# Quantizing x's row tiles every 18 pieces from step 127 on, in place of once per unit

## The reference

```python
xn = layernorm(x)                       # x: 4 x 512 x 512
s = attention(xn, wq, wk, wv, wo)       # 32 query heads of 16, one key and value head, causal
h = linear8bit(xn, W1, b1)              # 512 -> 2048
g = silu(linear8bit(h, W2, b2))         # 2048 -> 512
out = x + s * g
```

## Time and profile before

| | |
|---|---|
| median of 3 runs | 774.07 us (772.74 to 776.4) |
| profiled execution | 773.78 us |
| its span, first to last instruction | 772.1 us |
| TensorE busy | 736.0 us (95%) |
| VectorE busy | 635.6 us (82%) |
| ScalarE busy | 398.3 us (52%) |
| GpSimd busy | 295.6 us (38%) |
| granted TensorE clock, mean | 0.997 |

### The profile page before, as it was taken

The page is one execution under the profiler, slowest core; times in us unless marked ns, Lnnn a source line. Parts: engine busy times, 40 slices in busy tenths (PEclk is TensorE's granted clock), DMA queues, the critical chain, the costliest instruction groups (busy, mean ns, idle before and its releaser), DMA issues. The chain is left out here.

```text
span 772.1 us, 11989 instructions
## 1 busy us (share of the span) xinstructions
PE 736.0 (95%) x4133; PEld 560.6 (73%) x4133; DVE 635.6 (82%) x1080; ACT 398.3 (52%) x681; POOL 295.6 (38%) x369
## 2 busy tenths in 40 slices
PE   4998999999999999999999999999998999999995
PEld 3887765656666777765678878788876888888884
DVE  7878999998999999995548588597869998599957
ACT  4653566766676777777634445454463333132312
POOL 7557445555555555554622222122100000127404
PEclk9999999999999999999999999999999999999998
DMA  7542123222323333344455766555315588337972
GB/s 259 161 168 60 40 54 88 72 73 85 85 85 91 97 90 90 86 122 144 145 191 155 205 218 183 184 118 151 83 44 195 199 257 271 124 93 252 323 287 109
DMA packets 93772, 110.71 MB, mean 143 GB/s; under 512 B 43136, under 2 KB 50320, under 8 KB 92176
## 3 DMA queue, kind: packets, MB, share of 16 engines
q1 hardware_dynamic: 93712, 109.95, 46.8%
HBM read 56.43 MB, written 40.37 MB: 125 GB/s over the span
## 5 line engine op out<-in xcount | busy, mean ns | idle before, releaser
L1024 DVE TENSOR_REDUCE rowmax<-ps 128x2 f32<-128x512 f32 (+3 forms) x384 | 211.5, 589 | 20.4 <-PE ps L1137 18.0
L946 ACT ACTIVATE probs<-ps 128x512 f32<-128x512 f32 (+1 forms) x352 | 174.4, 561 | 66.5 <-PE ps L1152 65.3
L1137 PE MATMUL ps<-km,stack 128*128 128x256 f32 (+3 forms) x512 | 142.5, 325 | 2.8 <-PEq L236 2.1
L1152 PE MATMUL ps<-stack,ks 128*128 128x512 f32 (+1 forms) x352 | 131.8, 383 | 4.4 <-ACT probs L946 3.4
L1137 PEld LDWEIGHTS ps<-km,stack 128*128 128x128 f32 (+1 forms) x512 | 92.2, 189 | 36.6 <-DVE rowmax L1024 19.4
L899 POOL TENSOR_SCALAR_AFFINE_SELECT probs<-probs 128x512 f32<-128x512 f32 x128 | 80.6, 638 | 55.8 <-ACT probs L946 55.0
L2019 PE MATMUL ps<-big_h 128*128 128x512 f32 x256 | 100.0, 390 | 2.0 <-DVE big_l L1835 1.6
L2020 PE MATMUL ps<-big_l,big_h 128*128 128x512 f32 x256 | 99.6, 389 | 0.0
L2021 PE MATMUL ps<-big_h,big_l 128*128 128x512 f32 x256 | 99.6, 389 | 0.0
L1167 PE MATMUL ps<-probs,vones 128*32 128x512 f32 (+3 forms) x1024 | 82.2, 439 | 0.2 <-POOL probs L899 0.2
L1152 PEld LDWEIGHTS ps<-stack,ks 128*128 128x128 f32 x352 | 66.4, 189 | 14.4 <-ACT probs L946 7.2
(11 more groups left out here) (234 smaller groups left out, 1377.6 us busy)
## 6 DMA issues: line engine op xcount, KB each, us to landing
stack<-big_h SPq DMA_DIRECT2D x128, 64.0 KB, 2.0
h_scratch<-hs SPq DMA_DIRECT2D x7, 1024.0 KB, 4.7
hload<-h_scratch SPq DMA_DIRECT2D x14, 512.0 KB, 5.3
xn_scratch<-xa SPq DMA_DIRECT2D x4, 1024.0 KB, 4.6
stack<-big_l SPq DMA_DIRECT2D x64, 64.0 KB, 2.0
xi<-xn_scratch SPq DMA_DIRECT2D x16, 256.0 KB, 2.7
xe_scratch<-xm SPq DMA_DIRECT2D x16, 256.0 KB, 2.3
w2n<-in_L_ffn_W_dram SPq DMA_DIRECT2D x4, 1024.0 KB, 6.7
```

The costliest lines, as they stand in the source:

```text
L946: nc.scalar.activation(probs[p][:, o:o + nh * w], ps[:, STB[n % NST], 0:nh * w], ACT.Exp).then_inc(s_exp, 1)
L1024: nc.vector.tensor_reduce(dst, src, AX_X, ALU.max).then_inc(s_red, 1)
L1137: last = nc.tensor.matmul(dst, stack[u % 3][rows, hp, P * qt:P * (qt + 1)], km[rows, u // KT, p0:p0 + npar, keys], start=True, stop=True)
L1152: ins = nc.tensor.matmul(ps[:, STB[n % NST], 0:nh * w].rearrange("p (h q) -> p h q", h=nh), ks[:, u // KT, p, P * kt:P * (kt + 1)], stack[ ...
```

## The change

The tiles no longer go with the units. Tile i is loaded at step 128 + 18i, masked at 136 + 18i, scaled at 139 to 142 + 18i, rounded at 143 + 18i, scaled back at 145 + 18i and stored at 147 + 18i. The reload of a stored tile in the tail (line 825) follows the last store. Engines, operations, buffers and semaphores stay.

```diff
--- before.py
+++ after.py
@@ -645,7 +645,8 @@
         PV_AT = {11: (0, 0), 16: (0, 1), 22: (1, 0), 27: (1, 1)}
         NORM_AT = {19: 0, 27: 1, 30: 2, 33: 3}
         SHARE_AT, HIGH_AT, LOW_AT = 30, 34, 33
-        XLOAD_AT, XMASK_AT, XSCALE_AT, XROUND_AT, XBACK_AT, XSTORE_AT = -1, 15, 21, 25, 26, 30
+        XFIRST, XSTEP = 127, 18
+        XLOAD_AT, XMASK_AT, XSCALE_AT, XROUND_AT, XBACK_AT, XSTORE_AT = 1, 9, 12, 16, 18, 20
 
         LATE_AT = {("kv", LAST, 0): 0, ("q", LAST, 0): 6, ("q", LAST, 1): 12, ("v", LAST, 0): 18,
                    ("q", LAST, 2): 18, ("q", LAST, 3): 24}
@@ -675,6 +676,10 @@
 
             t = g - CH - LAG - at
             return t // CH if t % CH == 0 and 0 <= t < CH * U else -1
+
+        def x_tile_at(g, at):
+            i, r = divmod(g - XFIRST - at, XSTEP)
+            return i if r == 0 and 0 <= i < NT else -1
 
         def maximized(g, after):
 
@@ -803,12 +808,12 @@
                 queries(1)
                 queries(2)
                 for g in range(STEPS):
-                    u = unit_at(g, XLOAD_AT)
+                    u = x_tile_at(g, XLOAD_AT)
                     if u >= 0:
                         if u:
                             sp.wait_ge(s_xt, u)
                         sp.dma_start(xi[:, :], xn_d[P * u:P * (u + 1), :]).then_inc(s_xl, 16)
-                    u = unit_at(g, XSTORE_AT)
+                    u = x_tile_at(g, XSTORE_AT)
                     if u >= 0:
                         sp.wait_ge(s_xe, u + 1)
                         sp.dma_start(xe_d[P * u:P * (u + 1), :], xm[:, :]).then_inc(s_xes, 16)
@@ -822,7 +827,7 @@
                         if i >= NPAIR:
                             sp.wait_ge(s_tt, i - NPAIR + 1)
                         sp.dma_start(tail_in(i), xe_d[P * i:P * (i + 1), :]).then_inc(s_tr[i % 2], 16)
-                    if unit_at(g, XSTORE_AT + 1) == U - 1:
+                    if x_tile_at(g, XSTORE_AT + 1) == NT - 1:
                         sp.wait_ge(s_xm, NT)
                         sp.wait_ge(s_xes, 16 * (EARLY + 1))
                         sp.dma_start(inlier_row[:, :], xe_d[P * EARLY:P * (EARLY + 1), :]).then_inc(s_xel[0], 16)
@@ -857,7 +862,7 @@
                     nc.gpsimd.tensor_tensor(big_l[:, k, rows], late_row(k), big_h[:, k, rows].bitcast(F32),
                                             ALU.subtract).then_inc(s_paf, 1)
                 for g in range(STEPS):
-                    u = unit_at(g, XMASK_AT)
+                    u = x_tile_at(g, XMASK_AT)
                     if u == 0:
                         pool.wait_ge(s_pah, high_at[("magic", 0, 0)] + 1)
                     if u >= 0:
@@ -866,7 +871,7 @@
                             pool.wait_ge(s_xes, 16 * u)
                         nc.gpsimd.tensor_tensor(xm[:, :], xi[:, :], inlier_row[:, :],
                                                 ALU.mult).then_inc(s_xm, 1)
-                    u = unit_at(g, XROUND_AT)
+                    u = x_tile_at(g, XROUND_AT)
                     if u >= 0:
                         pool.wait_ge(s_xt, u + 1)
                         nc.gpsimd.tensor_tensor(xm[:, :], xm[:, :], magic_row[:, :],
@@ -950,7 +955,7 @@
                         act.wait_ge(s_d2, 3 * (u + 1))
                         nc.scalar.copy(attended(big_h, u),
                                        tb[:, :, :].rearrange("p a b -> p (a b)")).then_inc(s_ah, 1)
-                    u = unit_at(g, XBACK_AT)
+                    u = x_tile_at(g, XBACK_AT)
                     if u >= 0:
                         act.wait_ge(s_xr, u + 1)
                         nc.scalar.mul(xm[:, :], xm[:, :], xs[:, 1:2]).then_inc(s_xe, 1)
@@ -1030,8 +1035,8 @@
                         if unit_at(g, at) >= 0:
                             normalize(unit_at(g, at), part)
                     for part in range(4):
-                        if unit_at(g, XSCALE_AT + part) >= 0:
-                            quantize_x(dve, unit_at(g, XSCALE_AT + part), part)
+                        if x_tile_at(g, XSCALE_AT + part) >= 0:
+                            quantize_x(dve, x_tile_at(g, XSCALE_AT + part), part)
                     i = tail_tile(g, 2)
                     if i >= 0:
                         dve.wait_ge(s_xh, i + 1)
```

## The result

| | before | changed |
|---|---|---|
| median | 774.85 us (beside it, on the same chip) | 794.93 us (792.94 to 795.74, 4 runs) |
| ratio to before | | 1.0253, 95% interval 1.0233 to 1.0273 |
| profiled span | 772.1 us | 794.0 us |

What follows compares the result with a forecast made beforehand. VectorE sets the pace in pieces 48 to 143, then TensorE, with no slack at three places a unit. Terms -3.4 + 3.75 + 3.4 + 1.35 + 2.2 = +7.3 on 773.8 gave 781 us, range 778 to 784.

Steps and rivals of the forecast that it cites:

- A rule weighed: VectorE operations with both inputs in SBUF and GpSimd instructions reading SBUF exclude one another; left out of the sum.
- the third rival: GpSimd holds up VectorE's last tile operation at places 8 to 11 and line 1078: 786 us, chance 0.1.
- Places 8 to 11: Tiles 4, 8, 12 scaled there delay the reduction of place 13, on which place 16 hangs: 0.45 each, +1.35 us.
- Places 14 to 17: Tiles 3, 7, 11: VectorE waits 0.55 for the mask, then delays place 17's reduction: 1.25 each, +3.75 us.
- Places 2 to 5: Four tiles scaled there delay the reduction of place 6, on which place 9 hangs: 0.85 each, +3.4 us.
- places 20 to 23: Tiles a step earlier than today cost nothing, covered by idle 0.51 us before place 23; otherwise 0.6 each.
- Relief: Before the output projection starts, VectorE has three tiles less and waits for ACT's exponentials go: -3.4 us.
- The last tile: In the tail its GpSimd rounding goes ahead of three selects, delaying TensorE's last product and the block's end: +2.2 us.

Runs made afterwards that it cites:

- the run with all four on one input: Changed kernel, last tile seven steps later, VectorE's scaling and unit-end maximum, rounding copy and subtraction replaced by one-input reductions: 782.46 us, ratio 1.009.
- the run with the relief alone: Kernel before the change, with VectorE's maximum and scaling of tiles 0 to 3 on one column instead of 512: 771.58 us, ratio 0.9946.
- the first experiment: Changed kernel, with every tile's two-input scaling on VectorE replaced by a one-input row maximum over the same 128x512 tile: 788.74 us, ratio 1.0163.

## Why the prediction was wrong in size

Pieces 168 to 359 took 13.8 us longer, not 7. The direction was right, and so was its ground: TensorE follows the reductions without slack at a few places, and the moved tiles delay these. With all four kinds of instruction on one input, three units lose 2.82 us (57.72 against 54.90); the prediction's positions sum to 2.55 for the same four tiles. As a sum the model of queues was good, in part by luck: one position was too dear and another too cheap, as below. What failed, step by step:

- **A rule weighed, and the third rival.** This is the failing step. The rows agreed with the rule, I wrote so, and still made the sum as if it did not hold, with 0.1 for a rival that priced it at 5.3 us. Measured: 8.9 us (282.43 less 273.50). The Trainium skill, SBUF — State Buffer, "Who interferes with whom", says that a row reduction never takes part in this on Trainium2, and counts copies and casts among those that can, under conditions on their operands; the runs agree, the copy 1.00 beside the rounding, the reduction in its place 0.17. My price took in only the scaling and 0.37 of line 1078. It left out the copy (0.67, four times), the maximum of the halves (0.44, at the same places) and the subtraction caught by the whole of a mask (1.04, three times), because I looked at which instruction the moved work would *be*, not at which ones its GpSimd part would be *beside*. The trace of before had shown two of them already: the maximum took 0.29 to 0.34 us in units 2 to 5 against 0.17 or 0.18 in the others, the copy 0.28 or more from unit 2 on against 0.17.
- **Places 8 to 11: +0.45 each.** By TensorE's weight loads, place by place against the units of before, the loss is 2.5 us a tile, 1.0 without exclusion (the run with all four on one input) and 0.4 with VectorE's work on the tile away too. That last part is ScalarE's wait for the rounding, which I had put at nothing beyond what TensorE had already lost. I also counted three such tiles; tile 0, at steps 139 to 142, is the fourth. Units 5 and 6 took 37.40 us in the run with all four on one input, against 16.57 and 18.52 of the run with the relief alone: 2.3, less tile 1's 0.8, so tile 0 costs 1.5 even without exclusion.
- **Places 14 to 17: +1.25 each.** Measured 1.6, by another mechanism: 1.04 of the subtraction instead of 0.55 of the wait. With the subtraction out of the way, the wait was there as written (0.55), and the loss was 1.0.
- **Places 2 to 5: +0.85, places 20 to 23: nothing.** Measured 0.86, and 0.3 at the beginning of unit 10, where the maximum of the halves takes 0.45 beside GpSimd's subtraction; without exclusion 0.8 and nothing.
- **Relief: -3.4.** Units 2 to 4 gave 2.31; with the 0.61 that unit 5 gave in the run with the relief alone (17.18 to 16.57) that is 2.9. In the changed kernel tile 0's cost covers unit 5's share, so pieces 48 to 143 took 67.6 us, not 65. In the run with the relief alone it is 0.58 a unit, less than the 0.77 of units 2 to 4 here; that run left the tiles' parts on GpSimd and ScalarE in place, and no run takes these away alone.
- **The last tile: +2.2.** Measured 3.24. The chain ran as written up to the last select, which ended 2.3 later than before (400.50 less 367.73, the start of the last piece, against 379.51 less 349.04). But what TensorE waited for was VectorE's transposition behind the tile, and its last product then ran at the lower clock level, 4.05 us against 2.14 and 0.43. At the upper level its first part would have ended at about 400.0 (397.88 and the 2.14 of the run with the last tile later, an estimate), and the select would have held the rest, as forecast; the clock made the difference.

Together: from unit 1 to the last piece the forecast had +5.1 (-3.4 + 3.75 + 3.4 + 1.35), and +16.4 was measured. Of the 11.3 between them 8.9 are exclusion. The other 2.4 are left with all four kinds on one input: 1.5 for tile 0, 0.5 in unit 15 (19.02 against 17.63 us, where 0.85 was forecast), 0.3 in units 7 to 14 (7.1 against 6.8), the rest is small. With the tail's 1.0 the forecast's 7.3 becomes 19.6, which is what the profiles differ by from unit 1 to the FFN.

## What to carry to other kernels

When an instruction moves, look up in the timeline what runs beside it on the other engine at the new place (here VectorE and GpSimd), for each of its parts and each neighbour: here three operations of 0.2 to 0.3 us at the end of a unit cost 5.0 us, as much as the moved scaling (4.7). A rule that the rows bear out belongs in the sum, not among the rivals. An operation on VectorE's critical path can be written as a reduction of one input: in these runs such reductions were not held by GpSimd in any unit. A period that isn't that of the unit brings several positions in turn, here four, and the one shift that was tried only chose which of them collide.

## What the runs showed of the hardware that was not expected

- A held instruction ended less than one normal duration after the other had ended: scaling 0.55 behind GpSimd's subtraction (on one column 0.02), copy 0.03 and subtraction 0.05 behind the rounding and the mask. GpSimd's next instructions were then longer in turn (two selects 1.68 instead of 1.23).
- A 128x512 row maximum in the middle of GpSimd's subtraction kept its 0.68 us (the first experiment, at 224.59).
- After the same idle time of 2.1 us at the block's beginning, the granted clock from 66.5 to 70.5 us was 0.57 to 0.67 in eight of the fourteen profiles (the changed kernel's is one) and 1.00 in six (the one with the last tile later is one). Unit 0 takes 18.2 to 18.3 us in the eight and 16.7 to 16.8 in the six. The eight reach piece 0 at 66.5 us or later, the six at 66.3 or earlier; what decides it stays open.
